# Scoring both heads of a pair together, with their correction passes on 64-row tiles side by side

## The reference

```
xn, latn = layernorm(ctx), layernorm(layernorm(x))
q = latn @ Wq;  k, v = split(concat([xn, latn]) @ Wkv)          # heads of 64
weight = softmax(q k^T / 8);  out = (weight v) @ Wo;  x = x + out
```

## Time and profile before

| | |
|---|---|
| median of three runs | 1582.4 us (1577.87 to 1582.47) |
| the profiled execution's own time | 1578.58 us |
| span of its trace, first to last instruction | 1576.9 us |
| mean granted TensorE clock | 0.966 of 2.4 GHz |
| first attention: first score to last matmul | 26.8 to 693.6 us |
| a plain pair step (first score to first score) | 9.36 us |
| the step r = 2, with the output projection | 15.19 us |

### The profile page before, as it was taken

One profiled execution on the slowest core, in us unless ns is written; L12 is line 12 of the kernel. 1 busy time (PEld: TensorE's weight loads), 2 busy tenths in 40 slices (PEclk: granted clock), 3 DMA queues, 4 the chain that ended last, 5 costly groups with the idle time before them and its releaser, 6 DMA issues. The chain is left out here.

```text
span 1576.9 us, 28767 instructions
## 1 busy us (share of the span) xinstructions
PE 1454.4 (92%) x10026; PEld 1198.4 (76%) x10026; DVE 946.8 (60%) x1762; ACT 883.6 (56%) x2198; POOL 651.6 (41%) x956
## 2 busy tenths in 40 slices
PE   7999999999999999969899999899997569999995
PEld 5878787878787878748789988676665248888885
DVE  4776767676767676746411114888888644444542
ACT  4886878777867687734311113676774224444442
POOL 7514444444343433050511003546321035877774
PEclk8999999999999999979999999899999779999998
DMA  5400000000000000010589993100000513444442
GB/s 173 138 2 21 1 22 1 18 6 1 21 2 21 2 1 1 1 32 3 204 297 315 318 316 93 28 14 17 13 1 2 166 54 109 125 121 125 123 114 27
DMA packets 74449, 120.29 MB, mean 76 GB/s; under 512 B 7008, under 2 KB 55136, under 8 KB 74304
## 3 DMA queue, kind: packets, MB, share of 16 engines
q1 hardware_dynamic: 63600, 101.76, 19.8%
q0 software_dynamic: 10704, 16.65, 5.2%
HBM read 99.78 MB, written 18.61 MB: 75 GB/s over the span
## 5 line engine op out<-in xcount | busy, mean ns | idle before, releaser
L519 ACT ACTIVATE a_p<-a_s,a_negmax 128x512 f32<-128x512 f32 x256 | 176.2, 688 | 110.4 <-DVE a_negmax L647 61.0
L647 DVE TENSOR_REDUCE a_negmax<-a_s 128x1 f32<-128x512 f32 x256 | 176.3, 689 | 74.6 <-PE a_s L380 70.7
L279 POOL TENSOR_TENSOR a_o_l<-a_o,a_o_h 128x256 fp32r<-128x256 f32 x64 | 47.0, 736 | 296.9 <-ACT a_o_h L544 296.9
L389 PEld LDWEIGHTS a_t<-ident,a_p 128*128 128x128 f32 x1024 | 122.4, 140 | 50.7 <-issue 22.8
L389 PE MATMUL a_t<-ident,a_p 128*128 128x128 f32 x1024 | 157.0, 276 | 0.7 <-DVE a_pT L662 0.7
L1708 ACT ACTIVATE h_probs<-h_scores,h_negmax 128x256 f32<-128x256 f32 x256 | 118.2, 478 | 65.8 <-DVE h_negmax L1898 65.8
L2203 POOL TENSOR_TENSOR n_w_l<-n_raw,n_w_h 128x768 fp32r<-128x768 f32 x64 | 118.2, 1847 | 74.4 <-ACT n_w_h L2246 74.4
L407 PE MATMUL a_out_p<-a_pT,a_v 128*64 128x256 f32 x1024 | 124.6, 385 | 0.0
L379 PE MATMUL a_s<-a_k_hl,a_q_hh 128*128 128x512 f32 x256 | 105.9, 414 | 2.3 <-issue 1.5
L2385 DVE TENSOR_TENSOR n_hidden<-n_up,n_silu 128x512 f32<-128x512 f32 x64 | 44.3, 693 | 98.3 <-PE n_up L2288 94.0
L380 PE MATMUL a_s<-a_k_hl,a_q_l 128*128 128x512 f32 x256 | 100.5, 393 | 0.0
(11 more groups left out here) (436 smaller groups left out, 4444.8 us busy)
## 6 DMA issues: line engine op xcount, KB each, us to landing
e_w_in<-in_L_ffn_gate_up_proj SPq DMA_DIRECT2D x31, 1024.0 KB, 6.9
n_raw<-in_L_ffn_w SPq DMA_DIRECT2D x64, 384.0 KB, 3.0
e_w_out<-in_L_ffn_down_proj SPq DMA_DIRECT2D x31, 512.0 KB, 5.4
rows_in<-a_zeros SPq DMA_DIRECT2D x1, 3968.0 KB, 15.2
e_rows<-rows_in SPq DMA_DIRECT2D x31, 128.0 KB, 5.1
rows_out<-spare POOLq DMA_DIRECT2D x31, 128.0 KB, 4.5
a_both<-in_ctx SPq DMA_DIRECT2D x8, 256.0 KB, 2.7
a_both<-in_x SPq DMA_DIRECT2D x8, 256.0 KB, 3.0
```

The lines of the kernel that those rows point to most:

```text
L389: ins = pe.transpose(turned_p[j % 2][:, c, :], probs[j][:, c * P:(c + 1) * P], g.ident[:, :])
L519: act.activation(probs[j][:, :], scores[j % 2][:, :], ACT.Exp, bias=negmax[:, j:j + 1], accum_out=total[:, r % 2, j % 2, j // 2:j // 2 + 1 ...
L647: dve.tensor_reduce(negmax[:, j:j + 1], scores[j % 2][:, :], AX.X, ALU.max, negate=True).then_inc(max_set, 1)
```

## The change

A block's number now means: j // 2 is the half of the queries, j % 2 the head. `score(b, r, t)` scores both heads for one half t of the queries: two full passes (one head each, into the two PSUM tiles), and then the two low passes on the 64 rows that carry something, head 0 on rows 0 to 63 and head 1 on rows 64 to 127. There are two such calls per pair. The order of the four engines that take part changes to fit, and all four turns of a pair now come in its own step, so that the calls behind the last step go.

```diff
-                def score(b, r, j):
-                    h, rows = j // 2, slice(j % 2 * P, (j % 2 + 1) * P)
-                    if j == 0:
+                def score(b, r, t):
+                    rows = slice(t * P, (t + 1) * P)
+                    if t == 0:
                         pe.wait_ge(ql_set, PAIRS * b + r + 1)
                         pe.wait_ge(kl_set, PAIRS * b + r + 1)
-                    wait(pe, exp_set, 4 * (PAIRS * b + r) + j - 1)
-                    pe.matmul(scores[j % 2][:, :], q_hh[r % 2][:, h, rows], k_hl[r % 2][h][:, :], start=True, stop=False)
-                    pe.matmul(scores[j % 2][:, :], q_l[r % 2][:, h, rows], k_hl[r % 2][h][:, :],
-                              start=False, stop=True).then_inc(s_done, 1)
+                    for h in range(2):
+                        wait(pe, exp_set, 4 * (PAIRS * b + r) + 2 * t + h - 1)
+                        pe.matmul(scores[h][:, :], q_hh[r % 2][:, h, rows], k_hl[r % 2][h][:, :], start=True, stop=False)
+                    for h, half in enumerate(halves):
+                        pe.matmul(scores[h][:, :], q_l[r % 2][half, h, rows], k_hl[r % 2][h][half, :],
+                                  start=False, stop=True).then_inc(s_done, 1)
...
                         score(b, r, 0)
-                        if prev:
-                            turn(*prev, 2)
                         if nxt:
                             project_k(*nxt, first and bp == 0)
-                        score(b, r, 1)
-                        if prev:
-                            turn(*prev, 3)
-                        if nxt:
...
                             project_q(*nxt)
-                        score(b, r, 2)
                         turn(b, r, 0)
+                        turn(b, r, 1)
+                        score(b, r, 1)
...
-                        score(b, r, 3)
                         if prev:
                             attend(*prev)
-                        turn(b, r, 1)
+                        turn(b, r, 2)
+                        turn(b, r, 3)
```

More of the change, by code:

```diff
@@ L476, in _ @@
                 batches(pe, NB, step)
-                turn(NB - 1, PAIRS - 1, 2)
-                turn(NB - 1, PAIRS - 1, 3)
                 attend(NB - 1, PAIRS - 1)
@@ L519, in exponent @@
                     act.activation(probs[j][:, :], scores[j % 2][:, :], ACT.Exp, bias=negmax[:, j:j + 1],
-                                   accum_out=total[:, r % 2, j % 2, j // 2:j // 2 + 1]).then_inc(exp_set, 1)
+                                   accum_out=total[:, r % 2, j // 2, j % 2:j % 2 + 1]).then_inc(exp_set, 1)
                 def spread(b, r):
@@ L536, in set_even @@
                     wait(act, o_done, s - 1)
-                    act.activation(probsT[r % 2][j // 2][:, :, 0:P], turned_p[0][:, :, :], ACT.Copy).then_inc(even_set, 1)
+                    act.activation(probsT[r % 2][0][:, :, j // 2 * P:(j // 2 + 1) * P], turned_p[0][:, :, :], ACT.Copy).then_inc(even_set, 1)
                 def high_o(b, r):
@@ L549, in step @@
                         exponent(b, r, 0)
-                        if prev:
-                            set_even(*prev, 2)
                         if r == 6 and last < 2:
                             high_kv(b + 1, 1 - bp, 1)
+                        exponent(b, r, 1)
+                        if r == 5 and last < 2:
+                            high_kv(b + 1, 1 - bp, 0)
+                        set_even(b, r, 0)
+                        if prev:
+                            spread(*prev)
                         if nxt:
                             set_k(*nxt[:2])
[L556 to L561, removed]
                             set_q(*nxt[:2])
                         exponent(b, r, 2)
-                        set_even(b, r, 0)
                         exponent(b, r, 3)
+                        set_even(b, r, 2)
                         group = r // 2 + 1
@@ L587, in _ @@
                 batches(act, NB, step)
-                set_even(NB - 1, PAIRS - 1, 2)
                 spread(NB - 1, PAIRS - 1)
@@ L661, in set_odd @@
                     wait(dve, o_done, s - 1)
-                    dve.tensor_copy(probsT[r % 2][j // 2][:, :, P:2 * P], turned_p[1][:, :, :]).then_inc(odd_set, 1)
+                    dve.tensor_copy(probsT[r % 2][1][:, :, j // 2 * P:(j // 2 + 1) * P], turned_p[1][:, :, :]).then_inc(odd_set, 1)
                 def set_out(b, r):
@@ L681, in step @@
                         maximum(b, r, 0)
+                        maximum(b, r, 1)
                         if prev:
                             invert(*prev)
-                        maximum(b, r, 1)
-                        if prev:
-                            set_odd(*prev, 3)
+                        set_odd(b, r, 1)
+                        maximum(b, r, 2)
+                        maximum(b, r, 3)
                         if nxt:
                             low_k(*nxt[:2])
-                        maximum(b, r, 2)
-                        if nxt:
                             low_q(*nxt[:2])
-                        maximum(b, r, 3)
                         if prev:
                             set_out(*prev)
-                        set_odd(b, r, 1)
+                        set_odd(b, r, 3)
                         if r == 2 and not first:
@@ L710, in _ @@
                 invert(NB - 1, PAIRS - 1)
-                set_odd(NB - 1, PAIRS - 1, 3)
                 set_out(NB - 1, PAIRS - 1)
```

## The result

The changed kernel takes 1606.3 us (median of four runs, 1600.9 to 1609.8) against 1582.4 us; the ratio is 1.0145 with a 95% interval of 1.0113 to 1.0176, which is +23 us (18 to 28). It is slower, as forecast; the forecast was +15, 1597 us. The measured time lies in the range given for 8 in 10 (1582 to 1610) and at the upper end of the likeliest case's own (1588 to 1606). The profiled execution has 1604.6 us of span against 1576.9, +27.7 us. By stage: the first attention's last matmul ends at 717.0 us against 693.6, +23.5; the mixture behind it took 299.6 us against 294.7, +4.9; the rest is within 0.7 us. The mixture's code is the same in all kernels of this study, and its length in their seven profiles, one for each kernel, is spread from 293.3 to 299.6 us: 293.3 to 295.8 in the three with the old order, 296.8 to 299.6 in the four with the new one.

What follows compares the result with a forecast made beforehand. TensorE's queue in the first attention was taken as the bound; +17 us for tile switches, -3 at r = 5 and 6, +1 for first and last step gave +15, 1597 us against 1582.4; 8 in 10: 1582 to 1610.

Steps and rivals of the forecast that it cites:

- the likeliest case: The forecast itself, 1597 us at a chance of 0.70, with an excursion price of 0.33 to 0.40 us.
- Going in and out: TensorE entering and leaving 64-row tiles in `score`: 0.36 us per excursion against 0.23 saved, +17 us over 128 calls.
- (1): The last full matmul ahead of a tiled one takes longer on TensorE: +0.09 us.
- (2) and (3): First tiled pair, weight load uncovered, +0.10 to 0.11 us; last tiled pair before a full matmul, +0.09 to 0.10; taken as additive.
- rival B: Only part of the switch is paid: loads hidden, 1574 us, or two pieces overlapping, 1584; chance 0.12.
- (4): The first full matmul behind tiles takes longer on TensorE: +0.08 us.
- The order in plain steps: Nothing waits in a plain step of 9.63 us; turn 0 has 0.5 us to spare, turn 1 0.3.
- r = 6: Turn 1 waits about 0.5 us, `project_v`'s old wait goes; with r = 5, about -3 us over seven batches.
- The stage's edges: First and last step: turn 2 waits for its exponential in the first, up to +1.6 us, taken as +1.
- A: The change from 128 rows to two tiles of 64 is free: 1551 us, chance 0.06.
- D: The two tiles of the low passes don't run side by side: 1626 us, chance 0.02.
- C: TensorE begins to wait for exponentials, 0.4 us in some 56 steps, adding 22 us: 1619 us, chance 0.10.

Runs made afterwards that it cites:

- the second experiment: The kernel before, in the old order, with each of the 256 low passes run alone on its 64 rows; 1658.7 us, ratio 1.0488.
- the third: The changed kernel with the tiled pair of low passes issued twice in a row; 1630.4 us, ratio 1.0322.

## Why the prediction was right, and its size not

*What bounds the kernel.* Right. TensorE's queue set the stage's end before and after, and what the steps took longer came out at the end: 23.1 us by the steps, 23.9 by the medians.

*Going in and out.* The mechanism held in all four pieces, for 64 rows as for 32. Measured, as medians over the plain steps, against a score of full passes: (1) +0.09; (2) and (3) together +0.19, so additive, which was my choice against rival B; (4) +0.11 before `project_k` and +0.10 before `project_v`, where I had +0.08. That is the mis-sized piece. I took it from 1097.04, a single place, behind column tiles and not behind row tiles, though the load at (2) is the same kind of load and costs 0.10. The sum is 0.39 us, not 0.36, and net of the 0.23 saved +0.16 and not +0.13: 128 x 0.16 = 21 us where the forecast had 17. A further 0.03 us per step (2 us) is spread over the other matmuls: the five later ones of `project_k` sum to 1.17 us against 1.15. No run takes that apart.

*The order in plain steps.* Right: 9.35 us without tiles. Turn 1 and turn 3 kept their room.

*r = 6.* As forecast. Reckoned from a step with 0.36 on top the seven steps give back 3.6 us; I had 3. The wait of turn 1 is there, 0.35 us where the walk had 0.5, behind `high_kv` and the second exponential:

```profile
343.16 0.62 ACT L484 ACTIVATE a_kvT_h<-a_full 128x512 fp32r<-128x512 f32 x1
343.69 0.68 ACT L516 ACTIVATE a_p<-a_s,a_negmax 128x512 f32<-128x512 f32 x1
344.51 0.66 PE L393 MATMUL a_t<-ident,a_p 128*128 128x128 f32 x4 [0.35 <-ACT a_p L516]
```

*The stage's edges.* This is the term of the sum that was furthest off. I had +1 us for the first step; it is +2.2 beyond the 0.36. Turn 2 waits there for its exponential, as I said. I allowed up to 1.6 us and took 1; the gap is 1.46 us from start to start where it would be 0.12, so 1.34 us are lost:

```profile
33.70 0.28 PE L337 MATMUL a_v_p<-a_w_h,a_kvT_l 128*128 128x256 f32 x1
35.16 1.33 PE L393 MATMUL a_t<-ident,a_p 128*128 128x128 f32 x8 [1.18 <-ACT a_p L516]
```

What the +1 does not hold is the work itself: the first step now has four turns in place of two, which is 2 x 0.80 us for groups of eight matmuls against 2 x 0.35 for groups of four, +0.9. The end of the stage, where these turns stood, does not give them back: from the last pair's first score to the last matmul it takes 25.5 us before and after. Two more places were not in the sum at all: r = 6 of the last batch, +0.8, and the way back of the loop. There TensorE sat idle without a wait that the profile shows:

```profile
PE a_s L381 <- issue: 2.9, 1, 2.9
```

It was 1.5 us before, in the same view of the waits, and 1.7 in both other kernels with the old order; with the new order it is 2.6 to 3.5 in four kernels. Together the two steps at this place are +1.3 us over the plain price. Why the new order makes this idle time longer was not tested and stays open. The three are 4.3 us against 1. With 63 x 0.36 = 22.7 for the steps and -3.6 at r = 6 that is 23.4; the steps measure 23.1, and the stage, which started 0.4 later, 23.5.

*The rivals.* A (the switch is free, 1551) fell by the second experiment. B (loads hidden, or pieces 2 and 3 overlapping) fell by the third, where the first pair takes 0.34 and the last 0.33 while a lone pair takes 0.43. D fell by the third, where a pair costs 0.23. C, waiting in every step, did not come; the waits of `turn` on the exponential are 5.7 us in ten places:

```profile
PE a_t L393 <- ACT a_p L516: 5.7, 10, 1.6
```

## What to carry to other kernels

Row tiles halve the streaming of what is tiled and nothing else. Before using them, count the changes of shape in TensorE's queue, take a price for one from any tiled place in the trace (here 0.2 us in, 0.2 us out, between full-width matmuls), and ask how many tiled matmuls stand between two changes: at 0.23 us saved for each pair of 512 columns one pair loses, and two in a row would gain (0.46 against 0.39; an estimate, as no run here replaces four full passes by two pairs). And a step of the schedule that stands out in length, such as r = 6 here, is worth more than a rearrangement of all steps: one moved instruction on ScalarE gave 0.6%.

## What the runs showed of the hardware

A change of TensorE's tile shape had the same four pieces wherever it was seen, for 32 and 64 rows, for 64 columns and from row to column tiles: some 0.09 us on the last matmul ahead of it, a weight load that did not run ahead of the first tiled one, and the same two on the way out. The uncovered load is about 0.10 us for the 128 columns of the passes and projections, 0.06 for the turns behind tiles, and 0.05 with 64 columns: the first pair of attend's products takes 0.26 to 0.27 us, its neighbours 0.22. What I had not expected is that the matmul on half the rows costs the more for it even where its neighbour tile stays empty (0.35 us for each low pass, second experiment), and that rows-to-columns is no dearer than full-to-rows. And TensorE's idle time at the loop's way back was followed by 3.4 us at 1.2 GHz in four of the seven profiles (idle for 1.7, 2.6, 3.0 and 3.5 us) and not in three (1.5, 1.7 and 2.9), so the length of the idle time alone does not tell these apart.
